# Routing tables of a mixture-of-experts stage: other operand types, another layout, another order behind them

## The reference, cut to what matters

```python
x = x + tanh(g_xattn) * retention(layernorm(x), ctx, ctx, Wq, Wk, Wv)   # (8, 256, 256)
xf = layernorm(x).reshape(2048, 256)
scores = softmax(xf @ Wg.T)                       # 8 experts
w, idx = top_k(scores, 2); w = w / w.sum(-1, keepdims=True)
gates = (one_hot(idx, 8) * w[..., None]).sum(1)
h1 = lora_in(xf, W1, b1, A1, B1); h3 = lora_in(xf, W3, b3, A3, B3)   # per expert, 512 wide
y_e = lora_out(silu(h1) * h3, W2, b2, A2, B2)
x = x + tanh(g_ffn) * einsum('te,ted->td', gates, y_e)
```

## Time and profile before

| | us |
|---|---|
| median of three runs | 364.5 |
| the three runs | 364.54, 362.02, 364.5 |
| the profiled execution, its own time | 365.32 |
| its span, from the first to the last instruction | 363.5 |
| PE busy in the span | 305.6 |
| DVE busy in the span | 266.3 |
| POOL busy in the span | 192.6 |
| ACT busy in the span | 179.2 |

### The profile page before, as it was taken

How to read it: one execution, slowest core, us unless ns; L and a number is a source line. 1 busy time by engine, 2 the same in 40 slices (tenths; PEclk the granted TensorE clock), 3 DMA queues, 4 the chain that set the end, 5 groups by cost and what they waited for, 6 DMA issues and landing times.

```text
span 363.5 us, 7072 instructions
## 1 busy us (share of the span) xinstructions
PE 305.6 (84%) x1680; PEld 232.8 (64%) x1700; DVE 266.3 (73%) x638; ACT 179.2 (49%) x371; POOL 192.6 (53%) x169
## 2 busy tenths in 40 slices
PE   1959899899899760449999999999999999999980
PEld 1737677677677540326777777777777777777750
DVE  1577648888988569927888787778777778888750
ACT  4534436555555360116555555455555555555640
POOL 0547637777777571651555555455555555555331
PEclk9999679999999875559999999999999999999996
DMA  6779977686785445930333223333233233334200
GB/s 243 230 214 316 354 257 215 210 259 204 209 234 180 141 153 123 410 113 8 59 53 59 35 46 55 60 60 58 30 58 59 46 58 59 60 43 55 30 2 0
DMA packets 27903, 45.99 MB, mean 127 GB/s; under 512 B 6528, under 2 KB 15104, under 8 KB 27360
## 3 DMA queue, kind: packets, MB, share of 16 engines
q1 hardware_dynamic: 15408, 28.52, 24.8%
q0 software_dynamic: 7488, 9.36, 16.1%
q10 hardware_dynamic: 4976, 7.74, 6.9%
HBM read 33.65 MB, written 12.86 MB: 128 GB/s over the span
## 4 chain that ended last, share of the span: by engine, by line
PE 69%; DVE 7%; POOL 5%; DMA 5%; issue 5%; ACT 4%; SPq 1%; ACTq 1%; POOLq 1%; DVEq 0%
PE bank L474 29%; PE bank L491 15%; PE bank L482 5%; PE bank L418 4%; PE bank L384 3%; PE bank L464 2%; POOL WL L675 2%; DMA WH<-lora_in 2%; PE bank L340 2%; PE bank L411 2%; PE bank L393 1%; PE bank L429 1%; DMA LS<-lora_parts 1%; DVE WH L798 1%; ACT xn L563 1%
## 5 line engine op out<-in xcount | busy, mean ns | idle before, releaser
L734 POOL DMA_INDIRECT out<-ys,sidx x39 | 61.8, 1585 | 88.4 <-DVE gsel L974 58.0
L675 POOL TENSOR_TENSOR WL<-stage,WH 128x512 f32 (+1 forms) x48 | 60.3, 1273 | 33.9 <-ACT WH L558 33.9
L474 PE MATMUL bank<-WH,xh 128*128 x156 | 56.5, 443 | 0.7 <-ACT xh L633 0.7
L660 ACT ACTIVATE ys<-BB,gsel 128x256 f32 x39 | 19.9, 510 | 61.0 <-DMA out<-ys,sidx 57.0
L474 PE MATMUL bank<-WH,xl 128*128 x156 | 49.2, 397 | 0.0
L724 POOL DMA_INDIRECT xg<-xn_rows,gidx x39 | 38.7, 992 | 15.5 <-issue 11.3
L474 PE MATMUL bank<-WL,xb 128*128 x136 | 43.0, 386 | 1.6 <-issue 0.2
L558 ACT ACTIVATE WH<-stage 128x512 f32 (+1 forms) x48 | 29.0, 625 | 27.0 <-DVE stage L756 26.9
L989 DVE TENSOR_TENSOR h<-bank,BB 128x512 f32<-128x512 f32 x39 | 27.0, 691 | 17.3 <-PE bank L474 17.2
L984 DVE TENSOR_TENSOR gl<-bank,gh 128x512 fp32r<-128x512 f32 x39 | 27.0, 691 | 10.6 <-ACT gh L639 10.6
L639 ACT ACTIVATE gh<-bank 128x512 fp32r<-128x512 f32 x39 | 23.2, 596 | 23.1 <-PE bank L482 22.9
(11 more groups left out here) (127 smaller groups left out, 586.5 us busy)
## 6 DMA issues: line engine op xcount, KB each, us to landing
stage<-w_all_in SPq DMA_DIRECT2D x48, 256.0 KB, 3.5
BB<-biases_in SPq DMA_DIRECT2D x8, 640.0 KB, 9.0
LS<-lora_parts SPq DMA_DIRECT2D x24, 144.0 KB, 2.6
lora_parts<-WH ACTq DMA_DIRECT2D x3, 864.0 KB, 9.5
xs<-x_in SPq DMA_DIRECT2D x8, 256.0 KB, 3.5
cx<-ctxT_in SPq DMA_DIRECT2D x8, 256.0 KB, 3.5
out<-x ACTq DMA_DIRECT2D x8, 256.0 KB, 2.7
xn_rows<-xn ACTq DMA_DIRECT2D x8, 256.0 KB, 4.0
```

The costliest lines, as they stand in the source:

```text
L474: last = nc.tensor.matmul(dst[:, :], lhs[p][:, c * P:(c + 1) * P], W[:, bass.ds(e * (UNITS * UC) + (2 * kind + c) * UC, HID)], start=(part ...
L675: nc.gpsimd.tensor_tensor(w_dst(WL, s, m), stage[(u * UNITS + m) % NSTAGE][:], w_dst(WH, s, m).bitcast(F32), ALU.subtract).then_inc(s_wl, 1)
L734: nc.gpsimd.indirect_dma_start(out=out_rows, out_offset=bass.IndirectOffsetOnAxis(ap=sidx[:, i:i + 1], axis=0), in_=ys[p][:], in_offset=No ...
```

## The change

Four things are changed. The sources of the indicator and of BS are bf16 tiles (tiles_x, slots_x, hi_x, slf, tlf) in place of f32. The eight columns of a group lie innermost in AT, BS and these sources, so that DVE reads and writes unit steps, and PE reads its operands with a step of eight elements. The expanded sources are written by POOL ahead of time, in three copies that start when the last indices of the top two are there. The product with the column's number moves from POOL to DVE, and DVE writes all four indicators first, then the four products, then the four BS. The working out of each tile's expert moves behind gidx, and POOL's first three gathers wait for gidx alone (s_rows). s_routed and s_eid follow.

```diff
@@ -43,6 +43,7 @@
 KJ = K * NJ
+KQ = KJ // 4
 EPS = 1e-5
@@ -134,6 +135,7 @@
         route = ExitStack()
+        AT = sb(route, "AT", [P, 4, 3, NT_SLOTS, KQ], BF16)
         tri = sb(route, "tri", [P, P], BF16); ones = sb(route, "ones", [P, P], BF16)
@@ -141,16 +143,18 @@
         one8 = sb(route, "one8", [P, E])
-        Z = sb(route, "Z", [P, E, NJ]); PO = sb(route, "PO", [P, E, NJ])
-        PK = sb(route, "PK", [P, K, E, NJ]); pos = sb(route, "pos", [P, K, NJ])
+        Z = sb(route, "Z", [P, E, NJ])
+        PK = sb(route, "PK", [P, K, E, NJ]); PO = PK[:, 0]; pos = sb(route, "pos", [P, K, NJ])
         posi = sb(route, "posi", [P, KJ], I32); sli = sb(route, "sli", [P, KJ], I32)
         tli = sb(route, "tli", [P, KJ], I32)
-        slf = sb(route, "slf", [P, KJ]); tlf = sb(route, "tlf", [P, KJ])
-        AT = sb(route, "AT", [P, KJ, 3, NT_SLOTS], BF16)
-        BS = [sb(route, f"BS{i}", [P, KJ // 4, P], BF16) for i in range(2)]
+        slf = sb(route, "slf", [P, KJ], BF16); tlf = sb(route, "tlf", [P, KJ], BF16)
+        BS = [sb(route, f"BS{i}", [P, P, KQ], BF16) for i in range(2)]
+        slots_x = sb(route, "slots_x", [P, P, KQ], BF16); tiles_x = sb(route, "tiles_x", [P, NT_SLOTS, KQ], BF16)
+        hi_x = sb(route, "hi_x", [P, KJ], BF16)
         SV = sb(route, "SV", [P, 3, NT_SLOTS]); val = sb(route, "val", [P, NT_SLOTS])
         gof = sb(route, "gof", [P, NT_SLOTS]); nh = sb(route, "nh", [P, NT_SLOTS])
-        ET = sb(route, "ET", [1, NT_SLOTS, E]); ef = sb(route, "ef", [1, NT_SLOTS])
+        ET = slots_x[0:1].rearrange("p s w -> p (s w)")[:, 0:2 * NT_SLOTS * E].bitcast(F32).rearrange("p (i e) -> p i e", e=E)
+        ef = sb(route, "ef", [1, NT_SLOTS])
         dl = sb(route, "dl", [P, NJ]); e2 = sb(route, "e2", [P, NJ]); den = sb(route, "den", [P, NJ])
@@ -193,7 +197,8 @@
         s_H, s_rank, s_slots = sem("s_H"), sem("s_rank"), sem("s_slots")
-        s_ind, s_bs, s_atj, s_atp = sem("s_ind"), sem("s_bs"), sem("s_atj"), sem("s_atp")
+        s_ind, s_bs, s_atj, s_atp, s_grid = sem("s_ind"), sem("s_bs"), sem("s_atj"), sem("s_atp"), sem("s_grid")
+        s_rows, s_eid = sem("s_rows"), sem("s_eid")
         s_routed, s_e2, s_dl = sem("s_routed"), sem("s_e2"), sem("s_dl")
@@ -440,15 +445,15 @@
 
-            q = KJ // 4
             for kj in range(KJ):
-                if kj % q == 0:
-                    pe.wait_ge(s_bs, kj // q + 1)
-                    pe.wait_ge(s_atj, kj // q + 1)
-                    pe.wait_ge(s_atp, kj // q + 1)
-                last = nc.tensor.matmul(pV[:, 0:3 * NT_SLOTS], BS[kj // q % 2][:, kj % q, :],
-                                        AT[:, kj].rearrange("p a i -> p (a i)"), start=(kj == 0), stop=(kj == KJ - 1))
-                if kj % q == q - 1:
+                c, w = kj // KQ, kj % KQ
+                if w == 0:
+                    pe.wait_ge(s_bs, c + 1)
+                    pe.wait_ge(s_atj, c + 1)
+                    pe.wait_ge(s_atp, c + 1)
+                last = nc.tensor.matmul(pV[:, 0:3 * NT_SLOTS], BS[c % 2][:, :, w],
+                                        AT[:, c].rearrange("p a i w -> p (a i) w")[:, :, w], start=(kj == 0), stop=(kj == KJ - 1))
+                if w == KQ - 1:
                     last.then_inc(s_slots, 1)
@@ -515,7 +520,7 @@
 
-            pe.wait_ge(s_routed, 1)
+            pe.wait_ge(s_eid, 1)
             read_expert(0, 0)
@@ -618,11 +623,9 @@
             nc.scalar.activation(e2[:], dl[:], ACT.Exp).then_inc(s_e2, 1)
-            q = KJ // 4
             for c in range(4):
                 act.wait_ge(s_ind, c + 1)
-                nc.scalar.activation(AT[:, c * q:(c + 1) * q, 1, :], AT[:, c * q:(c + 1) * q, 2, :], ACT.Copy,
-                                     scale=cst[:, C_P:C_P + 1]).then_inc(s_atp, 1)
+                nc.scalar.activation(AT[:, c, 1], AT[:, c, 2], ACT.Copy, scale=cst[:, C_P:C_P + 1]).then_inc(s_atp, 1)
 
@@ -661,6 +664,7 @@
             act.wait_ge(s_routed, 1)
+            act.wait_ge(s_eid, 1)
             act.wait_ge(s_bb, 16 * E)
@@ -707,12 +711,11 @@
 
-            q = KJ // 4
-            for c in range(4):
-                pool.wait_ge(s_ind, c + 1)
-                nc.gpsimd.tensor_tensor(AT[:, c * q:(c + 1) * q, 0, :], AT[:, c * q:(c + 1) * q, 2, :],
-                                        cst[:, C_HI + c * q:C_HI + (c + 1) * q].unsqueeze(2).to_broadcast([P, q, NT_SLOTS]),
-                                        ALU.mult).then_inc(s_atj, 1)
+            pool.wait_ge(s_two, 2 * B)
+            pool.wait_ge(s_cst, 16)
+            nc.gpsimd.tensor_copy(tiles_x[:], cst[:, C_TILE:C_TILE + NT_SLOTS].unsqueeze(2).to_broadcast([P, NT_SLOTS, KQ]))
+            nc.gpsimd.tensor_copy(hi_x[:], cst[:, C_HI:C_HI + KJ])
+            nc.gpsimd.tensor_copy(slots_x[:], cst[:, C_IOTA:C_IOTA + P].unsqueeze(2).to_broadcast([P, P, KQ])).then_inc(s_grid, 1)
 
@@ -735,10 +738,11 @@
 
-            pool.wait_ge(s_routed, 1)
+            pool.wait_ge(s_rows, 1)
             pool.wait_ge(s_gates_d, 16)
             for i in range(XBUF - 1):
                 gather(i)
+            pool.wait_ge(s_routed, 1)
             for i in range(NT_SLOTS):
@@ -925,9 +929,9 @@
             then(nc.vector.tensor_tensor(Z[:], INC[:], CNT[:], ALU.subtract))
-            then(nc.vector.scalar_tensor_tensor(PO[:], base[:].unsqueeze(2).to_broadcast([P, E, NJ]), float(P), Z[:],
+            then(nc.vector.scalar_tensor_tensor(PO, base[:].unsqueeze(2).to_broadcast([P, E, NJ]), float(P), Z[:],
                                                 ALU.mult, ALU.add))
-            then(nc.vector.tensor_tensor(flat(Z), pK[:, 0:P], flat(PO), ALU.add))
+            then(nc.vector.tensor_tensor(flat(Z), pK[:, 0:P], PO.rearrange("p e j -> p (e j)"), ALU.add))
             for k in range(K):
@@ -938,28 +942,30 @@
             then(nc.vector.tensor_copy(tlf[:], tli[:]))
-            q = KJ // 4
+            dve.wait_ge(s_grid, 1)
+            part = lambda t, c, n: t[:, c * KQ:(c + 1) * KQ].unsqueeze(1).to_broadcast([P, n, KQ])
             for c in range(4):
-                r = slice(c * q, (c + 1) * q)
-                nc.vector.tensor_tensor(AT[:, r, 2, :], col(C_TILE, NT_SLOTS).unsqueeze(1).to_broadcast([P, q, NT_SLOTS]),
-                                        tlf[:, r].unsqueeze(2).to_broadcast([P, q, NT_SLOTS]), ALU.is_equal).then_inc(s_ind, 1)
+                nc.vector.tensor_tensor(AT[:, c, 2], tiles_x[:], part(tlf, c, NT_SLOTS), ALU.is_equal).then_inc(s_ind, 1)
+            for c in range(4):
+                dve.wait_ge(s_ind, c + 1)
+                nc.vector.tensor_tensor(AT[:, c, 0], AT[:, c, 2], part(hi_x, c, NT_SLOTS), ALU.mult).then_inc(s_atj, 1)
+            for c in range(4):
                 if c >= 2:
                     dve.wait_ge(s_slots, c - 1)
-                nc.vector.tensor_tensor(BS[c % 2][:], col(C_IOTA, P).unsqueeze(1).to_broadcast([P, q, P]),
-                                        slf[:, r].unsqueeze(2).to_broadcast([P, q, P]), ALU.is_equal).then_inc(s_bs, 1)
-
-            then(nc.vector.tensor_tensor(ET[:], cst[0:1, C_TILE:C_TILE + NT_SLOTS].unsqueeze(2).to_broadcast([1, NT_SLOTS, E]),
-                                         tend[0:1, :].unsqueeze(1).to_broadcast([1, NT_SLOTS, E]), ALU.is_ge))
-            then(nc.vector.reduce_sum(ef[:], ET[:], axis=AX))
-            then(nc.vector.tensor_scalar(eid[:], ef[:], float(E - 1), None, ALU.min))
+                nc.vector.tensor_tensor(BS[c % 2][:], slots_x[:], part(slf, c, P), ALU.is_equal).then_inc(s_bs, 1)
+
             dve.wait_ge(s_slots, 4)
             then(nc.vector.tensor_copy(SV[:].rearrange("p a i -> p (a i)"), pV[:, 0:3 * NT_SLOTS]))
             nc.vector.tensor_scalar(nh[:], SV[:, 2, :], -1.0, 1.0, ALU.mult, ALU.add)
             then(nc.vector.scalar_tensor_tensor(val[:], SV[:, 0, :], float(P), SV[:, 1, :], ALU.mult, ALU.add))
             then(nc.vector.tensor_scalar(is1[:], val[:], float(TOK), None, ALU.is_ge))
+            then(nc.vector.scalar_tensor_tensor(gof[:], is1[:], -float(TOK), val[:], ALU.mult, ALU.add))
+            nc.vector.tensor_copy(gidx[:], gof[:]).then_inc(s_rows, 1)
+            then(nc.vector.tensor_tensor(ET, cst[0:1, C_TILE:C_TILE + NT_SLOTS].unsqueeze(2).to_broadcast([1, NT_SLOTS, E]),
+                                         tend[0:1, :].unsqueeze(1).to_broadcast([1, NT_SLOTS, E]), ALU.is_ge))
+            then(nc.vector.reduce_sum(ef[:], ET, axis=AX))
+            nc.vector.tensor_scalar(eid[:], ef[:], float(E - 1), None, ALU.min).then_inc(s_eid, 1)
             nc.vector.tensor_scalar(is0[:], is1[:], -1.0, 1.0, ALU.mult, ALU.add)
-            then(nc.vector.scalar_tensor_tensor(gof[:], is1[:], -float(TOK), val[:], ALU.mult, ALU.add))
-            nc.vector.tensor_copy(gidx[:], gof[:])
             nc.vector.scalar_tensor_tensor(sidx[:], nh[:], col(C_PAD, 1), gof[:], ALU.mult, ALU.add).then_inc(s_routed, 1)
@@ -1016,6 +1022,7 @@
             dve.wait_ge(s_routed, 1)
+            dve.wait_ge(s_eid, 1)
```

## The result

The changed kernel took 365.57 us (median of 12 runs, 363.58 to 369.42), the kernel before 362.92 us in the same job (361.62 to 367.26): ratio 1.0094, 95% interval 1.0059 to 1.0129. It was measured twice more, beside the experiments: 1.0023 (0.9983 to 1.0063) and 1.0007 (0.9978 to 1.0036). The first ratio is clear of 1, the other two are not; all three lie under 1%, though the first one's interval reaches 1.3%. One profile can't say how much of the time is the change's: the first stage, the same code in all kernels, ended between 131.9 and 138.0 us in the executions that this text compares, and from the first xh to the end of the span, where the code hardly differs, they took 202.9 to 205.6 us (204.3 before, 205.4 changed). I therefore read the routing from the start of dl, DVE's first instruction of it, and name what lies behind by its length.

A forecast was written before the change was run, and what follows sets the result against it. DVE's chain was taken to pace the routing: tables -2.86 us, order -0.25, POOL's copies +1.9; then late bias broadcasts decide, xh 0.3 us later, so 364.5 + 0.3 = 364.8 us, range 361.5 to 367.0.

The forecast's parts named there:

- DVE's tables: Routing on DVE: bf16 and unit steps make a 312-element table cost 0.24 us and BS 0.61; SV 2.86 us earlier.
- Rival C: DVE's tables: bf16 forms miss the double rate with broadcast operands, BS 1.14 us each; +1.2 us, 365.7; chance 0.08.
- PE at "0.95 us, since no row shows a slower PE read": PE's matmuls in the routing: a group still takes 0.95 us though BS and AT are read with a step of eight.
- rival B: PE's matmuls in the routing: reads with a step of eight are slower; at 1.6 times +1.2 us, 365.7; chance 0.17.
- The 1.9 us delay all that DVE does: Routing from 138 on: DVE stands while POOL copies 1368 elements, 1.9 us, bounds nothing and 3.4 us.
- The bound of 3.4 us: POOL's copies in the routing: upper bound of their delay to DVE, at POOL's full 1.24 us for 512 elements.
- The gates' store and the broadcasts behind it: SP's queue: gate store moves from 139.55 to 141.45, the last bias broadcast lands 1.9 us later, at 158.3.
- So the broadcasts decide: Before the first tile: bias broadcasts end at 159.4, after the gather would allow xh at 159.0; xh at 159.5, 0.3 later.
- my 1 us for the gather among them: First gather among the bias broadcasts: issued at 154.12, lands 3.01 + 1 us later, at about 158.1.
- Behind SV: Between SV and the first gather: POOL no longer waits for sidx, which saves 0.25 us.
- The third stage: From 163 on: PE is busy 186.7 us of 190 at full clock, and the change touches nothing there.

The follow-up runs named there:

- grid_act: The changed kernel with the three copies of the expanded sources made by ACT in place of POOL; ratio to the kernel before 0.9978.
- at_outer: The changed kernel with only AT laid as before, columns outermost, so PE's moving operand is contiguous; ratio to the kernel before 0.9982.
- step4: The changed kernel with four columns innermost in AT in place of eight, PE's moving operand at a step of 8 bytes; ratio to the kernel before 0.9947.
- s4_late: The changed kernel with four columns innermost in AT, DVE's order by group, two copies on ACT, four experts' biases broadcast late; 359.29 us, ratio to the kernel before 0.9890.
- s4_inter: The changed kernel with four columns innermost in AT, the copies on ACT and DVE's order by group (indicator, BS, product); ratio to the kernel before 0.9978.
- s4_inter_bb: The changed kernel with four columns innermost in AT, copies on ACT, DVE's order by group, gates' store on ACT's queue; ratio to the kernel before 0.9960.

## Why the prediction was right or wrong

The forecast, a loss within noise (364.8 us against 364.5, within 1%), held, and 365.57 lies in the range. Partly this was luck: in the first job the loss was 2.65 us and not 0.3, in the traces 0.88, and three terms of the sum were off and nearly cancelled. Term by term:

- **DVE's tables.** 0.23 and 0.60 us from start to start, 0.24 and 0.61 taken. SV was to come 2.86 us earlier by them. Rival C is out.
- **PE at "0.95 us, since no row shows a slower PE read".** This step failed. A group took 1.75 us, 1.85 times, which is rival B. Its four groups cost 7.02 us and took back the whole gain: first indicator to SV 9.65 against 9.47. The Trainium skill's "Advanced Engine Details and Errata", section "SBUF Cachelines", asks for two accesses to each 16-byte line, and the runs agree: 7.02 us at one element for each line, 3.92 at two, 3.44 at eight (the last 0.4 us of this one at the higher clock, see below). It names no price and doesn't part the operands; the stationary one paid nearly nothing. I had the rule beside a row of DVE (1.6 times) and should have made it the likeliest case.
- **"The 1.9 us delay all that DVE does".** The mechanism is shown by grid_act, the size was 0.95. POOL's three copies ran from 133.90 to 135.68, about as long as I had taken; but tri, the two memsets and idxf on DVE still went through beside the first two (idxf with 0.27 us in place of 0.17), and mainly the OH, with two inputs in SBUF, waited out slots_x. The trace agrees here too with the exclusion that the Trainium skill states in "SBUF — State Buffer", section "Who interferes with whom". The bound of 3.4 us is 3.3 by its own price (1.24 us for 512 elements), which changes nothing.
- **The gates' store and the broadcasts behind it.** They did shift: the store from 2.35 to 3.30 us after dl's start, the last landing to 143.0 + 11.5 = 154.5, 20.7 after dl against 19.2 before: 1.5 us later where 1.9 was taken.
- **"So the broadcasts decide".** This step failed too. They didn't in the changed kernel, since PE's slowness kept the gather's rows behind them: xh at 156.69 is 2.2 us after their end. They decide as soon as PE is repaired. There my 1 us for the gather among them is 1.03 in at_outer but 2.9 in step4, since the last rows come only with the broadcasts' end, though asked for 5.7 us before it.
- **Behind SV** 0.25 us, exact.
- **The third stage.** 187.35 us busy of 190 against 186.71: untouched.

Sum of what happened: +0.95 (copies) + 0.18 (table) - 0.25 (order) = +0.88, as 22.88 - 22.00 in the traces. The forecast was +1.9 - 2.86 - 0.25 = -1.21, and +1.5 for the broadcasts, +0.3 in all. Its three errors were 3.04 us on PE, -0.95 on the copies and -1.5 on the broadcasts, which together make no more than 0.6.

## What to carry to other kernels

A layout that gives one engine unit steps gives another engine a step: price the reader before the writer. Here two elements for each 16 bytes kept both nearly fast (3.92 us on PE, 1.02 on DVE for four indicators). Before shortening a chain that ends in a small transfer, look for what fills the DMA engines at the time where it would move to; here two losses lay one behind the other, and neither repair alone brought much (0.27 us and nothing; 3.3 together). Where a first stage strays by some microseconds from run to run, compare stretches that start at a common instruction.

## What the runs showed of the hardware that I hadn't expected

- The step of the moving operand costs (7.02 us for 32 matmuls of 117 columns at 16 bytes, 3.44 contiguous), that of the stationary one hardly (6.83 with it contiguous and the moving one at 16 bytes).
- PE's granted clock stayed at 0.50 (1.2 GHz) through 7.00 us of gap-free matmuls with a step of 16 bytes. In at_outer it rose within the last 0.5 us of 3.4 us of matmuls with a contiguous moving operand, and was down again before the first tile, so it bought little. Whether it is the step that makes this difference is not shown; it is one execution. Windows of at_outer:

```profile
149.70:153.10 3.40, 3.40 (x32) 3.03 (x32) 1.89 (x3) 0.00 (x0) 0.00 (x0) 0.55 1.02 426
152.60:153.10 0.50, 0.50 (x7) 0.37 (x5) 0.00 (x0) 0.00 (x0) 0.00 (x0) 0.84 1.06 440
153.10:156.30 3.20, 0.00 (x1) 0.00 (x0) 2.50 (x11) 0.00 (x0) 1.29 (x2) 0.98 1.01 421
156.30:158.80 2.50, 0.02 (x1) 0.02 (x1) 0.00 (x0) 0.00 (x0) 1.89 (x3) 0.50 0.76 282
```

- POOL's first gather comes 0.29 us after the end of what releases it (gidx; sidx in the kernel before) wherever POOL had run a copy or product since its last subtraction, even one of 32 elements (s4_late), and 0.94 us after it in the two kernels where it had run none (grid_act, s4_inter). What it does in these 0.65 us wasn't tried. In s4_inter_bb the gates' store releases it, so it says nothing here.
- A gather among broadcasts got its last rows 0.2 and 0.5 us after they ended (step4, at_outer), and in step4 none of its packets ran in the first 3.4 us after its issue, while the broadcasts' filled the engines.
